# The scan stage of a MetaFormer block in chunks of 128 tokens and groups of 16 images, with the residual sum built by TensorE and evacuated by ScalarE

## What is computed

```python
Wx = batchnorm(x @ W.T)                      # over all images and tokens
yt = sigmoid(wx_t + yt @ V.T)                # for t in 0..3135, state (64 images, 128)
...
forget, inp, delta = sigmoid(z @ Wf + bf + 2), sigmoid(z @ Wi + bi), softplus(z @ Wd + bd) * 0.1
Ar, Ai, Br, Bi = spectra of 7x7 kernels, A bounded below 1
for _ in range(16):                          # complex state h, elementwise
    h = forget * (A * h) + delta * inp * (B * z)
```

## Time and profile before

| what | value |
|---|---|
| median of 3 executions | 16452.49 us (16402.66 to 16489.39) |
| the profiled execution, own time | 16475.65 us |
| its span | 16473.9 us |
| busy share PE, DVE, ACT, POOL over the span | 68%, 76%, 63%, 26% |
| mean granted TensorE clock | 0.763 of 2.4 GHz |

### The profile page before, as it was taken

How to read it: one execution, slowest core, us unless ns; L and a number is a source line. 1 busy time by engine, 2 the same in 40 slices (tenths; PEclk the granted TensorE clock), 3 DMA queues, 4 the chain that set the end, 5 groups by cost and what they waited for, 6 DMA issues and landing times. The chain is left out here.

```text
span 16473.9 us, 269631 instructions
## 1 busy us (share of the span) xinstructions
PE 11190.3 (68%) x86216; PEld 8358.9 (51%) x86216; DVE 12515.2 (76%) x28025; ACT 10361.8 (63%) x24318; POOL 4296.3 (26%) x4365
## 2 busy tenths in 40 slices
PE   7888888888887555555555555555555537777888
PEld 5666666666665333333333333333333315555788
DVE  6777777777774799999989899899989995554133
ACT  7888888888885555555555555555555547776200
POOL 4444444444443111111111111111111112211000
PEclk9999999999997666666666666666666666766555
DMA  3333333333332111111111111111111113333399
GB/s 73 80 80 84 86 86 80 80 80 81 86 85 63 34 39 40 38 38 41 38 38 40 38 38 40 38 38 38 41 38 38 33 28 95 95 93 85 103 314 313
DMA packets 2117075, 1191.51 MB, mean 72 GB/s; under 512 B 50565, under 2 KB 2098376, under 8 KB 2107604
## 3 DMA queue, kind: packets, MB, share of 16 engines
q1 hardware_dynamic: 1702548, 967.89, 23.4%
q10 hardware_dynamic: 409600, 205.55, 4.3%
q0 software_dynamic: 3648, 2.20, 0.0%
HBM read 708.85 MB, written 466.62 MB: 71 GB/s over the span
## 5 line engine op out<-in xcount | busy, mean ns | idle before, releaser
L1186 PEld LDWEIGHTS s_pW<-s_U,s_vh 128*128 128x128 f32 x6272 | 1445.6, 260 | 2499.3 <-ACT s_U L1077 2118.8
L1186 PE MATMUL s_pW<-s_U,s_vh 128*128 128x64 f32 x6272 | 1453.3, 325 | 1427.4 <-ACT s_U L1077 1424.8
L1077 ACT ACTIVATE s_U<-s_pW,s_zb 128x64 f32<-128x64 f32 x3136 | 981.5, 313 | 2126.3 <-PE s_pW L1186 2065.1
L1228 PE MATMUL s_pG<-s_wg,s_XNT 128*112 128x384 f32 x3584 | 1879.2, 614 | 5.2 <-ACT s_Z L1130 5.2
L831 POOL TENSOR_TENSOR s_rst<-s_var,s_epst 112x8 f32<-112x8 f32 x224 | 231.0, 1031 | 6063.5 <-DVE s_var L80 6063.5
L1095 ACT ACTIVATE s_XN<-s_X,s_nmr,s_rst 112x128 f32<-112x128 f32 x1792 | 735.0, 481 | 882.5 <-POOL s_nmr L835 882.5
L409 ACT ACTIVATE KB<-pV,qkb 32x392 f32<-32x392 f32 x2048 | 1189.8, 581 | 25.7 <-PE pV L499 1.9
L1221 PE MATMUL s_pN<-s_ident,s_XN 112*128 112x112 f32 x896 | 219.7, 401 | 1247.4 <-ACT s_XN L1095 1247.4
L1171 PE MATMUL s_pY<-s_ident,s_U 128*112 128x128 f32 x1792 | 414.1, 370 | 936.9 <-DVE s_X L950 936.7
L249 POOL TENSOR_TENSOR SS<-SS,mx 128x784 f32<-128x784 f32 x512 | 769.5, 1503 | 801.9 <-DVE mx L342 801.9
L1164 PE MATMUL s_pW<-s_XT,s_ws 128*128 128x448 f32 x896 | 789.1, 973 | 30.3 <-issue 29.6
(11 more groups left out here) (246 smaller groups left out, 34208.8 us busy)
## 6 DMA issues: line engine op xcount, KB each, us to landing
XL<-in_x_dram SPq DMA_DIRECT2D x64, 1568.0 KB, 12.4
XR<-in_x_dram SPq DMA_DIRECT2D x64, 1568.0 KB, 18.1
x_dram<-XR SPq DMA_DIRECT2D x64, 1568.0 KB, 8.1
xh_dram<-XH SPq DMA_DIRECT2D x64, 1568.0 KB, 8.1
s_X<-x_dram SPq DMA_DIRECT2D x224, 448.0 KB, 5.3
s_XQ<-xh_dram ACTq DMA_DIRECT2D x448, 224.0 KB, 2.7
x_dram<-s_IN SPq DMA_DIRECT2D x224, 448.0 KB, 4.0
r_X<-x_dram SPq DMA_DIRECT2D x64, 1568.0 KB, 14.2
```

The source lines that it names most:

```text
L1077: act.activation(U[j.par][:, t, :], pW[t // R % 2][:, B * (t % R):B * (t % R) + B], ACT.Tanh, bias=zb[:, 0:1], scale=0.5).then_inc(u_sb, 1)
L1186: pe.matmul(pW[t // R % 2][:, B * (t % R):B * (t % R) + B], vh[:], before, start=False, stop=True, skip_group_check=True).then_inc(z_ps, 1)
L1228: pe.matmul(pG[i % 3][0:T, 0:3 * C], XNT[:, i, :], wg[:], start=True, stop=True).then_inc(g_ps, 1)
```

## The change

In words:

- Chunks are 128 tokens (`TF`), so there are 25, the last of 64. Groups are 16 images (`OS`), so a chunk has 4 slots with K = 32 steps each, and there are 100 groups. Pieces of four images (`Q`) keep their size; there are NQ = 4 in a group. `inputs` takes R = 8 tokens.
- The loop over chunks is written out in full (`slots`); sizes are passed everywhere, for the short last chunk.
- Inputs and states share a tile, `XU`, channel x token x image: the matmul of inputs reads in order, and the copy of the transposed inputs writes with a stride.
- The residual sum: PE multiplies `X2` by the identity into `pY` and adds the states by matmuls with half the identity (`hident`); ACT copies the bank to `X2` (`residual`). DVE's sum (L950) is gone. For all but a chunk's first group this is done at k = 24 to 31 of the slot before.
- DVE takes the statistics first in its slot (in a chunk's first slot only behind `IN`); the product with `TG` for `Wv` is made earlier.
- `TG` has one buffer rather than two, `X2` three rather than four, and `XN` lies in the tile `f1`. So ACT's gates wait for DVE's ninth operation, DVE's writes to `f1` wait for the transposes of `XN`, and ACT's normalisation waits for the whole of the maths before.

The core of the diff:

```diff
+    TF = 128
+    OS = 16
+    NCH = (S + TF - 1) // TF
     NO = B // OS
-    SLOTS = 8
-    NX = 4
-    K = T // SLOTS
-    R = K // 2
+    NX = 3
+    K = TF // NO
+    R = 8
-    Q = OS // 2
+    Q = 4
+    NQ = OS // Q
...
-        XT = [sb(f"XT{i}", [C, B, T]) for i in range(2)]
-        U = [sb(f"U{i}", [C, T, B]) for i in range(2)]
+        XU = [sb(f"XU{i}", [C, TF, B]) for i in range(2)]
...
-        TG = [sb(f"TG{i}", [T, 4, OS, HC]) for i in range(2)]
+        TG = sb("TG", [TF, 4, OS, HC])
...
+        XN = pairs["f1"][:].rearrange("t r b c -> t (r b c)").rearrange("t (b c) -> t b c", b=OS)
...
+        def steps_at(j, s, k):
+            n = size(j) // NO
+            return [n * s + i for i in range(n) if i * K // n == k]
...
+            def load_x1(o):
+                c, s = divmod(o, NO)
+                wait(sp, dv, (o - NX + 1) * NV)
+                sp.dma_start(X2[o % NX][0:size(c)], tokens(x1_d, OS * s, OS, c)).then_inc(x2_ld[o % NX], 16)
...
-                            dve.scalar_tensor_tensor(v, pY[0:T, :].rearrange("t (b c) -> t b c", b=Q), 0.5, v,
-                                                     ALU.mult, ALU.add).then_inc(x2_d, 1)
...
+                if conv and s > 0:
+                    statistics(oc, tc)
...
+                if conv and s == 0:
+                    statistics(oc, tc)
+                if o is not None:
+                    after(7)
+                    turned_by(tm, Wv, inp, a, wp_d, wv_d, o)
...
+            def keep_turned(j, s, q):
...
+                act.copy(XU[n % 2][:, 0:size(n), b0:b0 + Q].rearrange("c t b -> c b t"),
+                         pX[:, 0:Q * size(n)].rearrange("c (b t) -> c b t", b=Q)).then_inc(xt_sb, 1)
+                load_xq(i + 2)
+
+            def residual(oc, q):
+                tc = size(oc // NO)
+                act.wait_ge(y_ps, oc * NQ + q + 1)
+                act.copy(X2[oc % NX][0:tc, Q * q:Q * q + Q, :].rearrange("t b c -> t (b c)"), pY[0:tc, :]).then_inc(x2_d, 1)
+
+            def gate(oc, tc, i):
+                act.wait_ge(g_ps, oc * OS + i + 1)
+                if i == 0:
+                    wait(act, dv, (oc - 1) * NV + 9)
...
+                    if conv and s == 0 and k in (1, 2, 3, 4):
+                        residual(oc, k - 1)
+                    if conv and s + 1 < NO and k in (25, 27, 29, 31):
+                        residual(oc + 1, (k - 25) // 2)
+                    if prep and k in (1, 4, 7, 10):
+                        keep_turned(j, s, k // 3)
+                    if conv and 10 <= k < 10 + NQ:
...
+                    if o is not None and k == 20:
+                        if conv:
+                            act.wait_ge(bx_d, oc + 1)
+                        act.activation(f1[:, 0], t1, ACT.Square, bias=cols[0:tm, 2:3]).then_inc(am, 1)
...
+            def turn_u(oc, q):
+                c, s = divmod(oc, NO)
+                tc = size(c)
+                wait(pe, x2_d, oc * NQ + q)
+                if q == 0:
+                    pe.wait_ge(x2_ld[oc % NX], (oc // NX + 1) * 16)
+                pe.matmul(pY[0:tc, :], ident[0:tc, 0:tc], X2[oc % NX][0:tc, Q * q:Q * q + Q, :].rearrange("t b c -> t (b c)"),
+                          start=True, stop=False, skip_group_check=True)
                 for i in range(Q):
-                    w = pe.transpose(pY[0:T, C * i:C * i + C], U[c.par][:, :, OS * s + Q * a + i], ident[:])
+                    w = pe.matmul(pY[0:tc, C * i:C * i + C], XU[c % 2][:, 0:tc, OS * s + Q * q + i], hident[:],
+                                  start=False, stop=True, skip_group_check=True)
                 w.then_inc(y_ps, 1)
...
+                    if conv and s == 0 and k < NQ:
+                        if k == 0:
+                            pe.wait_ge(u_sb, (j - 1) * TF + tc)
+                        turn_u(oc, k)
+                    if conv and s + 1 < NO and k in (24, 26, 28, 30):
+                        turn_u(oc + 1, (k - 24) // 2)
+                    if prep and k in (0, 3, 6, 9):
+                        turn_inputs(j, s, k // 3, oc)
+                    if conv and 11 <= k < 11 + NQ:
...
+                        turn_normal(oc, tc, k - 11)
+                    if conv and k >= K - OS:
...
```

More of the change, by code:

```diff
@@ L36 @@
 HID = 512
-OS = 8
 TOPK = 8
@@ L794, in _ @@
+            sp.wait_ge(x3_st, NGR * 16)
         @block.gpsimd
@@ L881, in _ @@
             dve.tensor_scalar(zb[:], zb[:], 0.5, None, ALU.mult).then_inc(dch, 1)
[L883 to L889 removed]
+            dve.tensor_scalar(hident[:], ident[:], 0.5, None, ALU.mult)
+            dve.memset(XU[1][:, TF - 1, :], -1.0).then_inc(ready, 1)
@@ new lines, in turned_by, with statistics @@
+                dve.tensor_tensor(flat(out[0:tc]), flat(out[0:tc]), flat(Dl[0:tc]), ALU.add).then_inc(sem_, 1)
+            def statistics(oc, tc):
+                dve.wait_ge(x2_d, oc * NQ + NQ)
+                wait(dve, ag_d, oc)
+                for i in range(OS):
+                    w = dve.bn_stats(st[0:tc, i, :], X2[oc % NX][0:tc, i, :])
+                w.then_inc(st_d, 1)
+                dve.wait_ge(st_d, oc + 1)
+                wait(dve, rs_d, oc)
+                moments(dve, st[0:tc], mean[0:tc], var[0:tc], tmp[0:tc], mo_d, oc * 2, ag_d, -0.5)
@@ new lines, in _, with after @@
+            for j, s, oc, o, scan, prep in slots():
+                if scan and s == NO - 2:
+                    spectrum(j)
+                conv = oc is not None
+                tc = size(oc // NO) if conv else 0
+                if conv and s > 0:
+                    statistics(oc, tc)
+                if o is not None:
+                    tm = size(o // NO)
+                    a = par_a[o // NO % 2]
+                    ar = a[0:tm, 0:HC].unsqueeze(1).broadcast_to([tm, OS, HC])
+                    a2 = a[0:tm, 4 * HC:5 * HC].unsqueeze(1).broadcast_to([tm, OS, HC])
+                    d0, t1, d1, t2, d2 = (half[n][0:tm] for n in ("d0", "t1", "d1", "t2", "d2"))
+                    f0, f1 = pairs["f0"][0:tm], pairs["f1"][0:tm]
+                    t0 = f0[:, 1]
+                    tf, ti = TG[0:tm, 0:2], TG[0:tm, 2:4]
+                    z, dl, bx, wv, inp = Z[0:tm], Dl[0:tm], BX[0:tm], Wv[0:tm], IN[0:tm]
+                    def after(n):
@@ L1044, in _ @@
+                if scan and s == NO - 2:
+                    bounded(j)
         @block.scalar
@@ new lines, in turn_normal @@
+            def turn_normal(oc, tc, q):
+                pe.wait_ge(xn_d, oc * NQ + q + 1)
+                wait(pe, n_sb, oc * NQ + q - 1)
+                for i in range(Q):
+                    w = pe.transpose(turned_bank[q % 2][:, tc * i:tc * i + tc], XN[0:tc, Q * q + i, :], ident[0:tc, 0:tc])
+                w.then_inc(n_ps, 1)
+            for j, s, oc, o, scan, prep in slots():
+                conv = oc is not None
+                tc = size(oc // NO) if conv else 0
+                if scan and s == 0:
+                    inputs(j, 0)
+                for k in range(K):
+                    if scan:
+                        for t in steps_at(j, s, k):
+                            wait(pe, u_sb, j * TF + t)
+                            before = XU[j % 2][:, t - 1, :] if t else XU[1 - j % 2][:, TF - 1, :]
```

681 lines of the change are left out of this document (306 added, 375 removed).

## The result

The changed kernel takes 14538.49 us (median of 4 runs, 14525.70 to 14561.95) against 16427.89 for the kernel before (4 runs beside it). The ratio is 0.8852, with a 95% interval of 0.8838 to 0.8867: 11.5% faster, where 9% was forecast. The time lies 42 us under the low end of the range. The profiled execution took 14537.58 us, with a span of 14535.8.

What follows compares the result with a forecast made beforehand. The bound was to move from DVE to the chain of steps over PE and ACT: 66 us a slot, scan ending at 12068 instead of 13577, so 14967, or 14945 against the median, stated as 14950 us; range 14580 to 15600.

Steps and rivals of the forecast that it cites:

- DVE's own work: DVE's operations in one slot of the scan, fixed parts and short waits between dependent operations included: 60.1 us.
- The last copy at 0.58 us: ACT's copy of 512 elements to X2 in the residual sum, at odd k from 24 to 31: 0.58 us.
- ACT's wait for POOL in a chunk's first slot: POOL's powers not ready by k = 10, as statistics run behind IN there: 1 to 2 us.
- the length of the loop: The PE, ACT, PE chain of recurrence steps with both engines' other work between: 258 us a chunk, 64.6 a slot.
- the term for k = 16 to 23: Eight steps of 0.86, one input matmul, three squares, and 2.4 for three steps at the low clock: 14.0 us.
- the 1.4 us added for the interplay of the two engines: Slot length put at 66 us, above 64 for DVE and 64.6 for PE and ACT, as each waits in places.
- The wait of DVE for the normalised states: DVE wants XN 26 us into its slot and gets it at 29 to 30: some 4 us of waiting.
- DVE alone: 61 us: Rival: high clock from k = 10 on and more hidden, so 61 us a slot, 14470 us; chance 0.11.
- The strided copy into XU: ACT's copy of transposed inputs, elements 256 bytes apart: taken at 0.6 us, bounds 0.6 and 1.0.
- The plain matmuls: 128-column matmuls adding states in k = 24 to 31, taken as twice four transposes: 2.2 us low clock, 1.4 high.
- The first rival: Product dearer or clock lower: k = 24 to 31 take 25 us, 72 us a slot, 15560 us; chance 0.20.
- The slower rival: Single buffer TG forms a ring of waits from k = 16: at 83 us a slot 16650 us; chance 0.04.

Runs made afterwards that it cites:

- e7: Changed kernel with six of the sixteen gate matmuls issued twice in each chunk's second slot: 14692.58 us, one execution.
- e6: Changed kernel with two unused DVE operations of 1024 elements added in each chunk's first slot: 14618.60 us, one execution.
- e2: Changed kernel with the product as four transposes a part, residual and half left out of the sum: 14485.97 us, one execution.
- e1: Changed kernel with the last eight DVE maths operations of a slot on a quarter of their elements: 14511.78 us, one execution.
- e5: Changed kernel with two unused DVE operations of 1024 elements added in each chunk's last slot: 14687.61 us, one execution.
- e8: Changed kernel with six of the sixteen gate matmuls issued twice in each chunk's last slot: 14667.07 us, one execution.
- e10: Changed kernel with unread matmuls of 384 columns on constants in PE's idle time at k = 0 to 15: 14452.58 us, ratio 0.8782.
- e9: Changed kernel with two DVE operations moved ahead of the wait for the normalised states: 14574.73 us, ratio 0.8863.

## Why the prediction fell short

**What held.** DVE's own work: 59.2 us a slot against 60.1. The clock in the scan, 0.75. The last copy at 0.58 us. The high clock from k = 19 on. ACT's wait for POOL in a chunk's first slot alone, though it was 5.95 us and not 1 to 2. DVE alone is the bound no longer: work on PE in the second slot cost its full price (e7), work on DVE in the first slot nothing (e6).

**The step that failed is the length of the loop, put at 64.6 us a slot where it was 62.3, and in it the term for k = 16 to 23; and behind it the 1.4 us added for the interplay of the two engines.** The steps of a middle slot by the starts of their tanh (8010.82, 8024.04, 8035.78, 8046.64, Exp at 8065.75, next slot 8072.29):

| part | forecast | measured |
|---|---|---|
| k = 0 to 9 | 13.5 | 13.2 |
| k = 10 to 15 | 12.4 | 11.7 |
| k = 16 to 23 | 14.0 | 10.9 |
| k = 24 to 31 | 18.7 | 19.1 |
| Exp, Ln, table loads | 6.5 | 6.5 |
| sum | 65.1 | 61.5 |

The forecast's 14.0 were eight steps of 0.86, 2.4 for the low clock, and 4.7 for an input matmul and three squares. That 4.7 is more than its own terms give: 0.9 for the inputs and three squares of 1.1 are 4.2, if nothing is hidden. The windows of the first three steps, k = 16, 17 and 18:

```profile
8035.78:8037.49 1.71, 1.71 (x5) 1.10 (x5) 1.68 (x2) 1.26 (x2) 0.00 (x0) 0.50 0.00 0
8037.49:8039.00 1.51, 1.51 (x5) 0.91 (x5) 1.51 (x1) 0.75 (x4) 0.00 (x0) 0.63 0.00 0
8039.00:8040.72 1.72, 1.72 (x7) 0.98 (x7) 1.72 (x3) 0.74 (x3) 0.00 (x0) 1.00 0.00 0
```

The clock was at its high level from k = 18 on, one step sooner than forecast, so the low clock cost (1.71 - 0.86) + (1.51 - 0.86) = 1.5 us and not 2.4. The step of k = 18 has the input matmul and cost 0.86 more. ACT's timeline shows what the squares cost:

```profile
8040.72 0.32 ACT L1107 ACTIVATE s_XU<-s_pW,s_zb 128x64 f32<-128x64 f32 x1 [0.98 <-PE s_pW L1236]
...
8041.59 0.32 ACT L1107 ACTIVATE s_XU<-s_pW,s_zb 128x64 f32<-128x64 f32 x1
8041.81 1.14 ACT L1153 ACTIVATE s_f<-s_t,s_cols 128x1024 f32<-128x1024 f32 x1
...
8043.26 0.34 ACT L1107 ACTIVATE s_XU<-s_pW,s_zb 128x64 f32<-128x64 f32 x1
...
8044.12 0.32 ACT L1107 ACTIVATE s_XU<-s_pW,s_zb 128x64 f32<-128x64 f32 x1
```

A step with a square takes 1.67 us (8041.59 to 8043.26) and one without 0.86: a square of 1.14 sticks out by 0.8. There are two such, and k = 19 to 23 take 5.92 = 5 x 0.86 + 1.6. The third stands at k = 16, where the step takes 1.71 us at the low clock, so that ACT's gap holds it. In place of 4.7 stand 0.86 + 1.6 = 2.5, and in place of 2.4 stand 1.5: these are the 3.1 us.

**The second error is the step from two lengths to one.** A chunk was forecast at 258 us (74, 65.1, 65.1, 54) and took 249.2 (76.5, 61.5, 61.5, 49.7). That is 62.3 a slot against 64.6. An error of the other sign is hidden in it: 5.95 us of the first slot are its wait for POOL, which the forecast put at 1 to 2 and left out of the 258. Then the forecast put 64 for DVE with its waits beside 64.6, and added 1.4 for what they cost each other: 66. Measured in full chunks are 61.4 for DVE with a short loop (e2), 62.3 for the loop with little of DVE (e1), and 62.3 for both. Nothing was added to the longer one, to within the half microsecond a slot by which the rise of the clock blurs such lengths. The wait of DVE for the normalised states that stood in the 64 was put at 4 us and was 2.1, and it was no separate cost: DVE waits because the loop is the longer one.

So of the 3.7 us a slot that were missed in full chunks, 2.3 are the loop's length and 1.4 the interplay. The 99 slots were forecast at 6510 us and took 6139, and with the slots before and behind them the scan ended 356 us sooner than forecast. The profiled execution ended 429 us sooner than its sum (14967). The other 73 are the part behind the scan, which nothing in the change touches: had it taken 2897 us as before, the time would be 14611, within the range. So the size of the miss is the sum's, and on which side of the range's low end it fell was chance. The time fell next to the rival "DVE alone: 61 us", and not by its mechanism: by e1 and e7 the loop binds, and by e5 DVE does in the last slot.

**Errors that were hidden.** The strided copy into XU took 1.05 us, the upper bound of the forecast and not 0.6. It cost nothing: the step that holds it still took 1.09 us (k = 1 to 2, 8011.91 to 8013.00), as ACT idled 0.78 us in a bare step and its next tanh began while the copy's record still had 0.18 us to go. The elements lie 256 bytes apart, and 512 of them took 1051 ns against 578 side by side. The Trainium skill (SBUF — State Buffer, Specifications) says that each crossing to a new 16-byte line pays a penalty. The trace agrees, with 1.8 times the time.

**The plain matmuls.** PE's timeline of one part of the product at 2.4 GHz:

```profile
8046.44 1.08 PE L1200 MATMUL s_pY<-s_X,s_ident 128*128 128x512 f32 x2
8047.35 1.81 PE L1203 MATMUL s_pY<-s_hident,s_XU 128*128 128x128 f32 x8
8049.00 0.81 PE L1265 MATMUL s_pG<-s_wg,s_XNT 128*128 128x384 f32 x2
```

They are recorded in pairs, as taken, but the eight took 1.81 us and not 1.4; the step took 3.37 against 3.2. Against the four transposes' 0.70 this is 2.6 times. The Trainium skill (TensorE: Matmul & The Clock Gate, Terms) gives transpose mode a factor of four for FP32; the trace does not show it here. The first rival took effect in part, since a plain matmul did cost more than two transposes. But k = 24 to 31 took 19.1 us and not 25, and the clock did not fall between the parts: it was 1.00 from k = 19 to 31.

The prediction says that the trace of the kernel before has no plain matmul of 128 columns. It has, in the attention part, where the clock was 1.00 (L560 is a transpose, L611 a plain matmul by the output weights):

```profile
2006.49 0.66 PE L560 MATMUL pT<-ident,On 128*128 128x128 f32 x4
2006.98 1.04 PE L611 MATMUL pT<-wp,OTs 128*112 128x128 f32 x8
```

Four plain ones took 1.04 us against 0.66 for four transposes, 1.6 times. This row spoke against the factor of four, and so against the first rival's price. Why the same work takes 1.81 in the scan is open; a difference between the two is that there the states are read 256 bytes apart.

**The slower rival.** The single buffer TG did not decide anything; ACT's waits show it:

```profile
ACT s_TG L1084 <- DVE s_Wv L1009: 3.6, 3, 1.2
```

The gates waited for DVE three times in 93 slots, 3.6 us in all.

What stays open is when the clock rises. The stretch from k = 16 to 24 takes between 10.8 and 12.1 us in the changed kernel, e5 and e8, all of the difference in k = 16 to 18, where the granted clock rises sooner or later (0.72 down to 0.57). In e10, which holds the clock up, those three steps took 3.72 us in every slot of full chunks, 3.79 once. So it is the clock that makes the difference; what moves the time of its rise by a microsecond no run shows.

## What to carry to other kernels

When two engines' chains come out within a few per cent of each other, price each by its own terms and take the longer one (here 62.3 and 61.4 us alone, 62.3 together): a pad on each and one on the sum is the same caution three times over. Compare such lengths over a stretch in which every period is alike, since a mean that takes in the last, unlike slots put 0.6 us on e1 that no full chunk had. A piece of work between steps costs only what sticks out of the slowest engine's step at that moment, so the same square is free at the low clock and costs 0.8 us at the high one. And before moving work to where an engine waits longest, ask whether the wait would turn up at the next hand-over: e9 moved 120 us of waiting and gained nothing.

## What the hardware showed that was not expected

Work that computes nothing made the kernel faster: with the constant matmuls in PE's idle time the granted clock rose from 0.75 to 0.96 and the pitch fell from 62.01 to 60.81 us. PE had been at 0.50 from k = 0 to 15, where steps and transposes leave it idle for 27% of the time (9.78 + 8.54 of 25 us busy), and had to come up in the gates.

The other surprise is how far a small shift carries. 2.3 us more of DVE work cost 3.4 a full chunk (e5), and some 4 us more of PE work in the last slot cost 3.4 where it had 2.5 us of slack (e8). In both the clock rose later in the first gates, 0.57 to 0.69 over k = 16 to 18 in place of 0.71 to 0.72, although PE's work there was the same.
